# Delta stage: one copy of the keys scaled by minus beta, and two groups of copies moved from VectorE to ScalarE

## The reference, cut to what matters

```
q, k = l2norm(h @ Wq), l2norm(h @ Wk);  v = h @ Wv;  beta = sigmoid(h @ Wb)
# chunk by chunk, carrying S:
kb = kc * bc[:, None]
A  = tril(kb @ kc.T, -1)
U  = solve_triangular(eye + A, vc * bc[:, None] - kb @ S, lower=True)
o  = qc @ S + tril(qc @ kc.T) @ U
S  = S + kc.T @ U
```

## Time and profile before

| | |
|---|---|
| time, median of 3 runs | 1392.16 us |
| profiled execution, its own time | 1395.43 us |
| profiled execution, first to last instruction (span) | 1393.5 us |
| busy in the span: PE, DVE, ACT, POOL | 997.9, 1099.6, 717.0, 789.7 us |
| mean granted clock of TensorE | 0.802 of full speed |

### The profile page before, as it was taken

How to read it: one execution, slowest core, us unless ns; L and a number is a source line. 1 busy time by engine, 2 the same in 40 slices (tenths; PEclk the granted TensorE clock), 3 DMA queues, 4 the chain that set the end, 5 groups by cost and what they waited for, 6 DMA issues and landing times.

```text
span 1393.5 us, 33043 instructions
## 1 busy us (share of the span) xinstructions
PE 997.9 (72%) x11963; PEld 732.8 (53%) x11963; DVE 1099.6 (79%) x3207; ACT 717.0 (51%) x1534; POOL 789.7 (57%) x670
## 2 busy tenths in 40 slices
PE   4547778677686546799999955656554699999960
PEld 1214455545555444678888842323232478788850
DVE  1188899989999894589788845898988689888845
ACT  2434253443534211467677735656565367677740
POOL 3331346556665544467777651158777747777650
PEclk9778778595876555699999986776676699999985
DMA  5010111111211104059778832122111659788839
GB/s 137 23 46 25 35 38 60 36 49 40 67 53 36 58 15 179 26 199 306 254 274 296 280 114 90 33 83 73 34 37 40 217 189 291 249 286 282 284 107 349
DMA packets 78625, 184.34 MB, mean 132 GB/s; under 512 B 16735, under 2 KB 44826, under 8 KB 68224
## 3 DMA queue, kind: packets, MB, share of 16 engines
q1 hardware_dynamic: 51280, 142.04, 30.5%
q0 software_dynamic: 17280, 35.70, 7.3%
q10 hardware_dynamic: 9904, 4.49, 1.2%
HBM read 131.20 MB, written 52.79 MB: 132 GB/s over the span
## 4 chain that ended last, share of the span: by engine, by line
PE 31%; DVE 28%; POOL 15%; issue 12%; ACT 7%; DMA 4%; SPq 1%; POOLq 0%; DVEq 0%; ACTq 0%
POOL xs L647 6%; PE ps L1594 5%; POOL res L690 5%; POOL rn L630 2%; PE ps L1810 2%; PE ps L1812 2%; PE ps L1811 2%; PE ps L1822 2%; PE ps L1824 2%; PE ps L1823 2%; DVE prod L817 2%; DVE t_p L821 2%; ACT ysc L1271 1%; DVE r_stats L739 1%; DVE hidl L1129 1%
## 5 line engine op out<-in xcount | busy, mean ns | idle before, releaser
L690 POOL DMA_INDIRECT res<-orow,idt x284 | 294.1, 1036 | 126.1 <-issue 80.6
L647 POOL DMA_INDIRECT xs<-ysc,slot_u x256 | 283.2, 1106 | 144.7 <-issue 72.8
L1129 DVE TENSOR_TENSOR hidl<-hidf,hidh 128x512 fp32r<-128x512 f32 (+1 forms) x320 | 199.1, 637 | 22.7 <-ACT hidh L1456 16.9
L1454 ACT ACTIVATE hidf<-ps,wb 128x512 f32<-128x512 f32 (+1 forms) x320 | 198.3, 655 | 5.0 <-PE ps L1812 4.4
L1810 PE MATMUL ps<-yTh,wb 128*128 128x512 f32 (+1 forms) x320 | 126.8, 396 | 0.0
L1822 PE MATMUL ps<-hidh,wb 128*128 128x512 f32 (+1 forms) x320 | 124.6, 389 | 0.0
L1812 PE MATMUL ps<-yTh,wb 128*128 128x512 f32 (+1 forms) x320 | 119.3, 373 | 0.0
L1811 PE MATMUL ps<-yTl,wb 128*128 128x512 f32 (+1 forms) x320 | 119.0, 372 | 0.0
L1824 PE MATMUL ps<-hidh,wb 128*128 128x512 f32 (+1 forms) x320 | 117.8, 368 | 0.0
L1823 PE MATMUL ps<-hidl,wb 128*128 128x512 f32 (+1 forms) x320 | 117.5, 367 | 0.0
L619 POOL TENSOR_TENSOR rstd<-rstd,neg_half 128x8 f32<-128x8 f32 x16 | 27.3, 1708 | 149.0 <-DVE rstd L746 149.0
(11 more groups left out here) (265 smaller groups left out, 2565.6 us busy)
## 6 DMA issues: line engine op xcount, KB each, us to landing
wb<-wblob SPq DMA_DIRECT2D x80, 1032.0 KB, 6.2
xt<-xs SPq DMA_DIRECT2D x62, 288.0 KB
wblob<-hl SPq DMA_DIRECT2D x16, 512.0 KB
fin<-res SPq DMA_DIRECT2D x14, 512.0 KB, 10.5
hidf<-res SPq DMA_DIRECT2D x10, 512.0 KB, 4.1
res<-orow,idt POOLq DMA_INDIRECT x284
xs<-ysc,slot_u POOLq DMA_INDIRECT x256
rs<-res SPq DMA_DIRECT2D x8, 512.0 KB, 4.3
```

The costliest lines, as they stand in the source:

```text
L647: pool.indirect_dma_start(xs[:, :], bass.IndirectOffsetOnAxis(slot_u[:, g % 2, k, n:n + 1], 0), ysc[:, g % 2, n, :], None).then_inc(s(f"mo ...
L690: pool.indirect_dma_start(res[m][:, :], bass.IndirectOffsetOnAxis(idt[:, t % IR, j:j + 1], 0), orow[:, t % OR, j, :], None, bounds_check=2 ...
L1129: ve.tensor_tensor(hidl[:, t % 2, c, 0:n], hidf[:, t % 2, c, 0:n], hidh[:, t % 2, c, 0:n].bitcast(F32), ALU.subtract)\
L1454: ins = act.activation(hidf[:, t % 2, c, 0:n], ps[:, c, 0:n], ACT.Gelu_apprx_tanh, bias=b_col)
```

## The change

Beta moves out of the right sides and out of the matrix's rows. A new tile kb = -beta times kn takes the place of kn as the weights of the Gram product and of the state's update, so the inverse is that of the matrix with beta on its columns, the right sides are plain v and kn, and the sign goes into vp (its operands are swapped). VectorE loses beta, the three R products and the four n_c products and gains one product, kb. ScalarE gains two copies for R and four for n_c; gp now waits for n_c's copy. TensorE gains a third set of transpositions through BK_A: kn, kb, qn in slots 22, 24 and 26. kn and qn now lie in the two halves of the tile sq, so both read `sq` in the lists below. The transposition n_p writes its output in order (128x1024) where it wrote it with a stride (128x32x32) before.

```
-        A_KQT = (22, 26)
+        A_KQT = (22, 24, 26)
# VectorE, stage_a
-                for k, (dst, c0, h0) in enumerate(((kn[:, g % 3], 0, 0), (qn[:, :, :], KW, HEADS))):
-                    if t == A_KN + k:
...
+                if t == A_KN:
...
+                    marks["beta"] = ch.mark(ve.tensor_scalar(nbeta[:, :, :], th[:, :, :], -0.5, -0.5, ALU.mult, ALU.add))
-                        ve.tensor_tensor(R[:, g % 2, hb, :, 0:DV], ... bc(beta[:, hb, :], 3, DV), ALU.mult)
-                    ve.tensor_tensor(R[:, g % 2, :, :, DV:RH], ... bc(beta[:, :, :], 3, DK), ALU.mult).then_inc(s("d_R"), 1)
+                if t == A_KN + 1:
+                    ch.wait(marks["beta"])
+                    ve.wait_ge(s("d_kn"), 3 * g + 1)
+                    ve.tensor_tensor(kb[:, g % 3]..., kn..., bc(nbeta[:, :, :], 3, DK), ALU.mult).then_inc(s("d_kn"), 1)
+                if t == A_KN + 2:
+                    ve.tensor_tensor(qn...).then_inc(s("d_kn"), 1)
                 if t in A_GRAM:
-                    ve.wait_ge(s("d_gram"), g * CG + c + 1)
+                    ve.wait_ge(s("d_nc"), g * CG + c + 1)
-                    ve.tensor_tensor(n_c[:, both]..., grams[:, :, :, 0], bc(nbeta[:, both]..., 3, C), ALU.mult)
# VectorE, row_of_inverse and stage_c
-                    ve.wait_ge(s("d_gp"), (g + 1) * CG)
-                    ve.transpose(n_p[:, :, :].rearrange("p i l -> p l i"), n_c...)
+                    ve.wait_ge(s("d_nc"), (g + 1) * CG)
+                    ve.transpose(n_p[:, :, :], n_c...)
-                        ve.tensor_tensor(by_pair(vp[:, at % 2]), by_pair(u[:, g % 2, both]), ps[:, 0:4, WS0:WS0 + 2 * DV],
+                        ve.tensor_tensor(by_pair(vp[:, at % 2]), ps[:, 0:4, WS0:WS0 + 2 * DV], by_pair(u[:, g % 2, both]),
# ScalarE, stage_a (z = 0, 1, 2: kn, kb, qn)
+                        if z == 1:
+                            act.copy(kT[:, :, :], turned).then_inc(s("d_kqTs"), 1)
                         else:
+                            if z == 2:
...
+                                act.copy(qT[:, g % 3], turned)
+                            for h in range(2):
+                                ins = act.activation(kqm[:, :, h, z // 2, :], turned, ACT.Copy, scale=head_of[:, h, 0:1])
+                if t == A_RV:
+                    act.wait_ge(s("d_kn"), 3 * g + 1)
...
+                    act.copy(R[:, g % 2, :, :, 0:DV], kqv[:, :, V0:V0 + HEADS * DV]...)
+                    act.copy(R[:, g % 2, :, :, DV:RH], kn...).then_inc(s("d_R"), 1)
+                if t in A_GRAM:
+                    act.wait_ge(s("d_gram"), g * CG + c + 1)
+                    act.wait_ge(s("d_inv"), g)
+                    act.copy(n_c[:, 2 * c:2 * c + 2]..., grams[:, :, :, 0]).then_inc(s("d_nc"), 1)
# TensorE
+                        src = (kn, kb[:, g % 3], qn)[z]
-                                ins = pe.matmul(ps[rows_of(a), j, KV0:KV0 + 2 * DV], kn[rows_of(j), g % 3, 2 * c + a // 2, cols],
+                                ins = pe.matmul(ps[rows_of(a), j, KV0:KV0 + 2 * DV], kb[rows_of(j), g % 3, 2 * c + a // 2, cols],
```

More of the change, by code:

```diff
@@ L211, in hybrid_kernel @@
         th = sb1("th", [BPB, HEADS])
[L212 removed]
         nbeta = sb1("nbeta", [BPB, HEADS])
         sq = sb1("sq", [BPB, KQ])
+        scaled = sq[:, :, :].rearrange("p n k -> p (n k)").rearrange("p (z n k) -> p z n k", z=2, n=BPB)
+        kn, qn = scaled[:, 0], scaled[:, 1]
         ss = sb1("ss", [BPB, 2 * HEADS])
         rn = sb1("rn", [BPB, 2 * HEADS])
[L217 removed]
         kT = sb1("kT", [CG, P])
@@ L777, in stage_a @@
-                if t == A_RV:
-                    ve.tensor_scalar(beta[:, :, :], th[:, :, :], 0.5, 0.5, ALU.mult, ALU.add)
-                    marks["beta"] = ch.mark(ve.tensor_scalar(nbeta[:, :, :], th[:, :, :], -0.5, -0.5, ALU.mult, ALU.add))
-                for half in range(GPB):
-                    hb = slice(half * GB, (half + 1) * GB)
-                    if t == A_RV + half:
-                        ch.wait(marks["beta"])
-                        if g >= 2:
-                            ve.wait_ge(s("d_uwp"), (g - 1) * CG)
-                        ve.tensor_tensor(R[:, g % 2, hb, :, 0:DV],
-                                         kqv[:, hb, V0:V0 + HEADS * DV].rearrange("p n (h d) -> p n h d", d=DV),
-                                         bc(beta[:, hb, :], 3, DV), ALU.mult)
@@ L793, in stage_a @@
                 if t in A_GRAM:
                     c = A_GRAM.index(t)
-                    ve.wait_ge(s("d_gram"), g * CG + c + 1)
+                    ve.wait_ge(s("d_nc"), g * CG + c + 1)
                     both = slice(2 * c, 2 * c + 2)
                     grams = ps[:, 0:4, 0:P].rearrange("p b (h z t) -> p b h z t", h=2, z=2)
-                    ve.tensor_tensor(n_c[:, both].rearrange("p n (a h) t -> p (n a) h t", h=2), grams[:, :, :, 0],
-                                     bc(nbeta[:, both].rearrange("p n (a h) -> p (n a) h", h=2), 3, C), ALU.mult)
@@ L808, in row_of_inverse @@
                 if t == 0 and step == 0:
-                    ve.wait_ge(s("d_gp"), (g + 1) * CG)
-                    ve.transpose(n_p[:, :, :].rearrange("p i l -> p l i"), n_c[:, :, :, :].rearrange("p n h j -> p j (n h)")).then_inc(s("d_np"), 1)
+                    ve.wait_ge(s("d_nc"), (g + 1) * CG)
+                    ve.transpose(n_p[:, :, :], n_c[:, :, :, :].rearrange("p n h j -> p j (n h)")).then_inc(s("d_np"), 1)
                 if 1 <= i < SUB and step == 0:
@@ L1313, in stage_a @@
                     act.wait_ge(s("d_ss"), g)
+                    act.wait_ge(s("d_kqT"), 3 * g)
+                    act.wait_ge(s("d_R"), g)
                     act.activation(sq[:, hb], kqv[:, hb, 0:KQ], ACT.Square).then_inc(s("d_sq"), 1)
-                for z in range(2):
+                for z in range(3):
                     if t == A_KQT[z] + 1:
-                        act.wait_ge(s("d_kqT"), 2 * g + z + 1)
+                        act.wait_ge(s("d_kqT"), 3 * g + z + 1)
                         act.wait_ge(s("d_gp"), g * CG)
@@ L1321, in stage_a @@
                         turned = ps[:, BK_A, :].rearrange("p (c t) -> p c t", t=P)
[L1322 to L1330 removed]
+                        if z == 1:
+                            act.copy(kT[:, :, :], turned).then_inc(s("d_kqTs"), 1)
+                        else:
+                            if z == 2:
+                                if g >= 3:
+                                    act.wait_ge(s("d_o"), (g - 2) * CG)
+                                act.copy(qT[:, g % 3], turned)
+                            for h in range(2):
+                                ins = act.activation(kqm[:, :, h, z // 2, :], turned, ACT.Copy, scale=head_of[:, h, 0:1])
+                            ins.then_inc(s("d_kqTs"), 1)
+                if t == A_RV:
+                    act.wait_ge(s("d_kn"), 3 * g + 1)
+                    if g >= 2:
+                        act.wait_ge(s("d_uwp"), (g - 1) * CG)
+                    act.copy(R[:, g % 2, :, :, 0:DV], kqv[:, :, V0:V0 + HEADS * DV].rearrange("p n (h d) -> p n h d", d=DV))
+                    act.copy(R[:, g % 2, :, :, DV:RH], kn.rearrange("p n (h d) -> p n h d", d=DK)).then_inc(s("d_R"), 1)
+                if t in A_GRAM:
+                    c = A_GRAM.index(t)
+                    act.wait_ge(s("d_gram"), g * CG + c + 1)
+                    act.wait_ge(s("d_inv"), g)
+                    grams = ps[:, 0:4, 0:P].rearrange("p b (h z t) -> p b h z t", h=2, z=2)
+                    act.copy(n_c[:, 2 * c:2 * c + 2].rearrange("p n (a h) t -> p (n a) h t", h=2),
+                             grams[:, :, :, 0]).then_inc(s("d_nc"), 1)
             def applied(g, c):
```

44 lines of the change are left out of this document (18 added, 26 removed).

## The result

The changed kernel takes 1408.61 us (median of 4 runs, 1405.92 to 1410.70) against 1393.15 us for the kernel before in the same session (1390.52 to 1396.40): a ratio of 1.0104, 95% interval 1.0076 to 1.0131. It is slower by 15 us where I forecast 6.6. The profiled execution of after has a span of 1407.9 us, before 1393.5: +14.4, of which 13.6 us are there at the n_p that ends pass 5 (474.11 and 487.71).

What follows compares the result with a forecast made beforehand. A string of passes, bound by VectorE up to vp, then by the path to the first convolution: +3.14 (passes -2, -1), +0.93 (pass 0), +5.00 (1 to 4), -1.06 (5), -1.4 (n_p): +6.6, 1398.8 us; 8-in-10 range 1390 to 1405.

Steps and rivals of the forecast that it cites:

- the terms ahead of the convolution: n_p to vp: kb and nbeta add 0.69 us in passes 1 to 5, 0.37 in pass 0; vp to first convolution +0.21.
- those of passes -2 and -1: Kn to first convolution: R copies and kT stand ahead of qn's transposition, +1.40 us in each pass.
- nothing is won there: Vp to first convolution: VectorE's earlier S brings no gain, its products stand behind qn's transposition and end before 277.35.
- some tenths earlier or later with the clock: Seven first convolutions: their ends may each shift some tenths with the clock; the reason given for the range 1395 to 1403.
- 0.21 a pass: Vp to first convolution: R copies ahead of kT on ScalarE delay the convolution's start by 0.21 us, bounds 0 to +1.6.
- the clock as a rival: First convolutions, passes -2 to 4: kb's transposition raises the clock earlier; up to 2.06 us each, 1384.4, half 1391.6; chance 0.07.
- Pass 5, -1.06 forecast: Pass 5, no convolution, VectorE taken as bound throughout: loses 2.10, gains 0.69, Gram products add 0.35, so -1.06 us.
- The Gram products, +2.4 forecast: t_c to n_p: handing n_c to ScalarE adds 0.35 us in passes 0 to 5, 0.17 in passes -2 and -1.
- the 0.17 that n_p was to win: n_p, now writing in order, falls from 2.09 to 1.92 us: -0.17 in eight passes, -1.4 in all.
- ScalarE's copies: Rival, slower: R copies take twice the forecast size, +1.4 us in passes -2 to 4, about +16, 1409; chance 0.05.
- The two faster rivals: VectorE bounds every pass, -4.6 us, 1387.6, chance 0.08; the clock rises earlier, 1384.4 or half 1391.6, chance 0.07.

Runs made afterwards that it cites:

- kb last: Changed kernel with nbeta and kb behind vp of slot 24, transpositions in the order kn, qn, kb, copies of R in slot 28: 1392.24 us, 0.9995.
- the idle time filled: Changed kernel with three extra 128x128 products, results unused, per group on TensorE in slots 26 and 29, ahead of the first convolution: 1400.05 us, 1.0044.
- padded before: Kernel before the change with 64 more instructions (long-met waits) at the head of TensorE's list: 1394.49 us, 1.0007.
- all its paddings: Changed kernel with extra long-met waits on TensorE: 64 at the head 1402.88 us, 128 1406.40, 192 1419.22; 64 there plus 128 in pass -2 1417.91.
- n_c on VectorE: Changed kernel with n_c copied by VectorE again in front of gp, no hand-over to ScalarE: 1407.10 us, 1.0099.
- the other bank: Changed kernel with kb's transposition in the odd projections' bank, so qn's transposition no longer waits for kT: 1403.69 us, 1.0069.
- the late convolution: Changed kernel with the first convolution behind kv and pv of slot 31 in TensorE's list, not in front of them: 1409.30 us, 1.0115.
- kb on GpSimd: The version with kb behind vp, its transposition last and R copies late, but nbeta and kb computed by GpSimd: 1400.64 us, 1.0048.
- the copies of R late: Changed kernel with ScalarE's two copies of R moved from slot 24 to slot 28, behind the queries' kqm: 1401.11 us, 1.0057.
- the four alignments: Changed kernel with 0, 64, 128 and 192 extra TensorE instructions, without the paddings' own time: 1408.6, 1402.9, 1404.6 and 1411.6 us.

## Why the prediction was wrong

The direction, the terms ahead of the convolution and those of passes -2 and -1 held: kb 0.68 ahead of vp, the convolution 6.05 behind vp and released by kqm, +1.44 in passes -2 and -1, n_p 1.95. The size did not: 15 us, not 6.6. What failed are terms that the sum put at nothing, and one gain that did not come. By steps:

*From the first convolution to t_c, for which the sum has no term: "nothing is won there", and the seven first convolutions only "some tenths earlier or later with the clock".* This is the step that failed most: it measured +4.1 us in passes 0 to 4. I counted what the copies of R do to the time at which the convolution starts, 0.21 a pass, and not what they do to TensorE in front of it. qn's transposition waits for kT, the products with S stand behind it, and TensorE was busy for 3.2 to 3.8 of the last 5 us in passes 1 to 4, before 3.8 to 4.2. The convolutions there went from 5.37 us in the mean to 6.10, with kb last (4.4 to 4.6 busy) to 4.39, and with the idle time filled to 4.52. I had the clock as a rival for the better only: kb's transposition gives TensorE more to do. Its work came, but with more waiting around it. Seven convolutions are 37.7 us before and 41.2 after; the other variants with after's order have 39.2 to 43.8 and padded before 38.2, so it is no accident of one execution, though single passes vary by 1.5 us. Nor does the busy time in front settle a single convolution: in before the one behind 4.14 us of work took 6.28 and the one behind 3.68 took 4.81. What is shown is the direction, in the means of passes 1 to 4, by the two edits that put more work or less waiting there. The Trainium skill, "TensorE: Matmul & The Clock Gate", section "What's actually happening", has activity release the throttle: the trace agrees, the same convolution at 0.55 behind waits and at 0.95 behind filled time.

*Pass 5, -1.06 forecast, since "there VectorE is the bound throughout".* It was not: vp to t_c is -0.25, not -2.10. VectorE's gain was met by GpSimd's ro, behind its sends and 4.23 us long. In before GpSimd waited 1.62 us for VectorE's ro, so there was at most that much room; I left it out. In after the six sends take 9.35 us, 8.34 before, so ro starts only 0.59 nearer to vp, and it takes 0.92 longer. Its length follows what VectorE does at its start. In the 17 traces ro runs 272 times. Where a VectorE product with both inputs in SBUF is under way, ro grows with what is left of it: 3.27 to 3.31 us with 0.51 left of gs, 4.20 to 4.26 with 1.44 to 1.50 left of n_c (31 of 31 cases). With no such product it takes 2.90 to 2.97, also beside x, which has one input in PSUM. In pass 5 of after, of all its paddings, of n_c on VectorE, the other bank, the filled time, the late convolution and kb on GpSimd, ro starts behind n_c's start (4.23 to 4.26); with the copies of R late it starts ahead of it (2.94), and with kb on VectorE and last it starts beside gs (3.30 or 3.31), and vp to t_c is 1.1 to 1.7 us shorter than before in these.

*TensorE's stops* were in no term. They cost n_p to kn 1.19 and 1.22 in passes 0 and 5 and 0.90 behind t_c in pass 1, and gave 0.91 and 0.50 back behind t_c in passes 0 and 3, where before had its own. The Trainium skill, "Runtime: NRT & Kernel Launch", section "Instruction fetch mechanics", has the instructions fetched in blocks of 256 while the current one runs, mostly hidden: the blocks agree with the 97 packets, the hiding doesn't hold in trains of 32x32 products, and 64 idle instructions at the head were worth 5.7 us, though the four alignments differ in the mean by only 1.7 us from the kernel as it is. What starts a packet early or late stays open: some start 1 us behind the block's first instruction, that of 439.96 only 5.8 us behind it.

*The Gram products, +2.4 forecast:* none. gp is 0.49 behind t_c, as I had it, but the stretch is paced by TensorE and the chain of four products, and n_c on VectorE again changed nothing that shows.

Of the 7.8 us between the forecast's 6.6 and the spans' 14.4: 4.1 first convolution to t_c, 1.9 pass 5, 2.7 n_p to kn in passes 0 and 5 (1.2 each, and the 0.17 that n_p was to win), 1.0 behind pass 5, and some tenths each in other terms, less 2.3 for the Gram products. The medians lie 1 us further apart than the spans because the profiled execution of before was 2.3 us above its median and that of after 1.1. Of the rivals, ScalarE's copies gave the right time (1409) by luck, for the wrong reason: they cost what I said (1.05 and 0.62 us), but what waits for them costs more. The two faster rivals fall: VectorE does not hold the convolution, which kqm releases, and the first convolutions got longer, not shorter.

## What to carry to other kernels

When a step is moved in front of a wait, follow not only who starts later but how long that one then runs: idle time of TensorE in front of a long product can be paid a second time in its clock, and removing it can be worth more than the step: with kb last the seven first convolutions took 33.6 us, 41.2 in after. An engine's saving is worth no more than the idle time of the engine that it hands over to. And measure a change of a few tenths of a per cent in two or three alignments of TensorE's instructions before believing its sign: 64 idle instructions moved the changed kernel by 0.4% and the one before by 0.1%, within its noise.
